# A small two-block image kernel: own shift products for two of four images, shared ones for the other two, fillers, halved last products and new engine orders

## The reference

```python
x = x + attention(_gn(x))   # qkv (1x1), 8 heads of 12 channels, l2-normalized q and k,
                            # 12x12 channel attention with temperature, softmax, projection + bias
x = x + ffn(_gn(x))         # 1x1 in, 8x8-patch real FFT times a filter, inverse FFT,
                            # 3x3 depthwise convolution, gelu(x1) * x2, 1x1 out
```

## Time and profile before

| | us |
|---|---|
| median of 3 runs | 68.55 (68.52 to 69.21) |
| profiled execution, its own time | 68.19 |
| span of its trace (first to last instruction) | 66.4 |
| TensorE busy | 59.0 |
| VectorE busy | 40.9 |
| ScalarE busy | 34.5 |
| GpSimd busy | 22.2 |

### The profile page before, as it was taken

The page is one execution under the profiler, slowest core; times in us unless marked ns, Lnnn a source line. Parts: engine busy times, 40 slices in busy tenths (PEclk is TensorE's granted clock), DMA queues, the critical chain, the costliest instruction groups (busy, mean ns, idle before and its releaser), DMA issues.

```text
span 66.4 us, 1346 instructions
## 1 busy us (share of the span) xinstructions
PE 59.0 (89%) x428; PEld 48.4 (73%) x428; DVE 40.9 (62%) x158; ACT 34.5 (52%) x88; POOL 22.2 (33%) x39
## 2 busy tenths in 40 slices
PE   3939999999999999999999999999999999979200
PEld 3929999979796989989899999889759651403000
DVE  0000035696416979699999859899998698870000
ACT  0710300037089466953519998968598614442920
POOL 3031003915160314330301599829397540000000
PEclk9999999999999999999999999999999999999999
DMA  0899999996000000000000000000000701520392
GB/s 0 239 340 268 368 239 260 247 262 197 25 0 0 5 0 0 0 0 10 0 0 5 0 0 0 10 0 0 15 5 20 236 11 35 149 93 0 83 307 84
DMA packets 3427, 5.83 MB, mean 88 GB/s; under 512 B 642, under 2 KB 1820, under 8 KB 3420
## 3 DMA queue, kind: packets, MB, share of 16 engines
q1 hardware_dynamic: 3004, 5.45, 28.8%
q10 hardware_dynamic: 416, 0.29, 1.9%
HBM read 4.04 MB, written 1.57 MB: 85 GB/s over the span
## 4 chain that ended last, share of the span: by engine, by line
PE 69%; DVE 7%; DMA 5%; ACT 4%; issue 3%; ACTq 1%; DVEq 1%; POOLq 1%; POOL 1%; SPq 1%
PE CH L735 26%; PE CV L735 18%; PE AB L735 15%; PE VB L735 10%; DMA XT<-in_xT 5%; DVE AB L723 3%; ACT X L538 2%; DVE AB L704 2%; DVE GT L729 2%; ACTq L272 1%; POOL CD L493 1%; POOLq L272 1%; DVEq L272 1%; ACT GE L578 1%; SPq L414 1%
## 5 line engine op out<-in xcount | busy, mean ns | idle before, releaser
L735 PE MATMUL AB<-CST,XT 128*97 128x128 f32 x64 | 9.4, 294 | 1.0 <-DMA XT<-in_xT 1.0
L486 POOL TENSOR_TENSOR ZP<-ZP,TURNED 128x512 f32<-128x512 f32 x6 | 7.6, 1271 | 5.9 <-ACT TURNED L533 5.8
L735 PEld LDWEIGHTS AB<-CST,XT 128*97 128x97 f32 x64 | 8.1, 178 | 1.3 <-DMA XT<-in_xT 1.3
L514 ACT ACTIVATE XF<-AB 97x512 f32<-97x512 f32 x8 | 4.7, 587 | 3.9 <-PE AB L735 3.9
L735 PEld LDWEIGHTS CH<-CST,ZA 128*128 128x128 f32 x48 | 5.8, 192 | 0.9 <-issue 0.8
L735 PE MATMUL CH<-CST,ZA 128*128 128x80 f32 x48 | 6.3, 275 | 0.0
L538 ACT ACTIVATE X<-CV,ST 96x512 f32<-96x512 f32 x6 | 3.8, 678 | 4.7 <-PE CV L735 4.7
L735 PE MATMUL CV<-X,AT 96*96 96x512 f32 x12 | 6.0, 597 | 0.0
L597 DVE COPY GI<-CH 97x97 f32<-97x97 f32 x2 | 0.5, 252 | 8.1 <-PE CH L735 8.1
L532 ACT ACTIVATE TURNED<-ZQ 64x512 f32<-64x512 f32 x6 | 3.8, 628 | 2.0 <-DVE ZQ L688 1.9
L475 POOL TENSOR_TENSOR RN<-NRM,POWER 96x2 f32<-96x2 f32 x4 | 2.8, 690 | 5.9 <-DVE NRM L639 5.9
(11 more groups left out here) (154 smaller groups left out, 130.2 us busy)
## 6 DMA issues: line engine op xcount, KB each, us to landing
X<-in_x SPq DMA_DIRECT2D x4, 384.0 KB, 8.3
out<-X SPq DMA_DIRECT2D x8, 192.0 KB, 2.2
XT<-in_xT SPq DMA_DIRECT2D x3, 388.0 KB, 6.3
XT<-in_xT SPq DMA_DIRECT2D x2, 194.0 KB, 3.2
WTS<-in_weights SPq DMA_DIRECT2D x1, 168.0 KB, 7.4
X<-GT SPq DMA_DIRECT2D x4, 32.0 KB, 1.9
WTS<-in_weights ACTq DMA_DIRECT2D x1, 126.9 KB, 5.4
LATE<-in_late SPq DMA_DIRECT2D x1, 109.5 KB, 6.8
```

The costliest lines, as they stand in the source:

```text
L486: ins = nc.gpsimd.tensor_tensor(ZP[:, b - 1, of], ZP[:, b - 1, of], TURNED[:, b - 1, of], ALU.add)
L514: nc.scalar.activation(XF[:, b, HALF * h:HALF * (h + 1)], bank[0:C1, :], ACT.Copy).then_inc(a_free, 1)
L735: return nc.tensor.matmul(o, lhsT, rhs, start=start, stop=stop)
```

## The change

Images 0 and 1 each get a shift product of their own (one SHIFT column each), so `shift.0` no longer waits for image 1's statistics. Images 2 and 3 share not only the shift but also the statistics product, the variance operations and the power. Two fillers (each one product of ones, two passes) stand before gram.1 and two more before attend.1. The final products of images 3 and 0 are issued half by half, each behind its own gate. All four orders are new: gram.0 comes ahead of spec.0.1, gram.2 and gram.3 behind shift.0.

```diff
 PE_ORDER = steps("""
-    spec.0.1 gram.0 gram.1 stats.0 gram.2 stats.1 gram.3 stats.2 shift.0 stats.3 spec.2.1 project.0
-    project.1 spec.1.0 logits.0 shift.2 logits.1 spec.3.1 softmax.0 project.2 setup.0 softmax.1 project.3
-    logits.2 spec.1.1 attend.0 logits.3 mix.0 attend.1 softmax.2 second.0 mix.1 spec.3.0 group.0 second.1
-    attend.2 spec.0.0 mix.2 group.1 softmax.3 fold.0 second.2 filter.0.0 group.2 spec.2.0 fold.1
-    filter.0.1 attend.3 filter.1.0 mix.3 fold.2 filter.1.1 edge.1.0 second.3 filter.2.0 edge.1.1 group.3
-    back.1.0 filter.2.1 back.1.1 edge.2.0 fold.3 edge.2.1 base.1.0 filter.3.0 filter.3.1 back.2.0
-    base.1.1 back.2.1 edge.3.0 final.1 edge.3.1 back.3.0 base.2.0 back.3.1 base.2.1 final.2 base.0.0
-    base.3.0 base.3.1 base.0.1 final.3 final.0
+    gram.0 spec.0.1 stats.0 fill.0 fill.0 gram.1 shift.0 gram.2 project.0 stats.1 gram.3 spec.0.0 stats.2
+    setup.0 logits.0 shift.1 spec.2.1 project.1 shift.2 softmax.0 logits.1 project.2 project.3 spec.2.0
+    attend.0 softmax.1 logits.2 mix.0 logits.3 second.0 fill.0 fill.0 attend.1 softmax.2 group.0 mix.1
+    spec.3.0 second.1 spec.1.0 softmax.3 attend.2 fold.0 group.1 mix.2 filter.0.0 second.2 filter.0.1
+    fold.1 spec.1.1 group.2 attend.3 filter.1.0 spec.3.1 filter.1.1 mix.3 fold.2 edge.1.0 second.3
+    filter.2.0 edge.1.1 group.3 back.1.0 filter.2.1 back.1.1 edge.2.0 fold.3 edge.2.1 filter.3.0 back.2.0
+    filter.3.1 base.1.0 back.2.1 edge.3.0 base.1.1 edge.3.1 final.1 back.3.0 base.2.0 back.3.1 base.2.1
+    final.2 base.0.0 base.3.0 base.0.1 base.3.1 final.3.0 final.3.1 final.0.0 final.0.1
 """)
 ACT_ORDER = steps("""
-    spec.0.1 shift.0 spec.2.1 tk.0 tk.1 shift.2 kl.0 spec.1.0 kl.1 tk.2 softmax.0 spec.3.1 tk.3 softmax.1
...
-    edge.3.0 final.1.0 final.1.1 edge.3.1 gelu.2.0 gelu.2.1 final.2.0 final.2.1 gelu.3.0 gelu.3.1
+    shift.0 tk.0 spec.0.1 spec.0.0 shift.1 tk.1 kl.0 shift.2 spec.2.1 softmax.0 tk.2 tk.3 kl.1 q1.0
...
+    swap.3.1 edge.3.0 edge.3.1 final.1.0 final.1.1 gelu.2.0 gelu.2.1 final.2.0 final.2.1 gelu.3.0
...
 DVE_ORDER = steps("""
-    gram.0 var.0 gram.1 var.1 gram.2 norm.0 norm.1 gram.3 var.2 var.3 norm.2 norm.3 project.0 project.1
...
-    gate.2.0 gate.2.1 rows.3 cols.3 gate.3.0 gate.3.1
+    gram.0 var.0 norm.0 gram.1 var.1 gram.2 gram.3 project.0 norm.1 var.2 logits.0 norm.2 rq.0 norm.3
...
+    gate.2.1 cols.3 rows.3 gate.3.0 gate.3.1
...
 POOL_ORDER = steps("""
-    var.0 var.1 var.2 var.3 logits.0 logits.1 logits.2 spread.0 logits.3 group.0 group.1 group.2 zsum.1.0
-    zsum.1.1 group.3 cdiff.1 rdiff.1 zsum.2.0 cdiff.2 zsum.2.1 zsum.3.0 rdiff.2 zsum.3.1 cdiff.3 rdiff.3
+    var.0 var.1 var.2 logits.0 logits.1 logits.2 logits.3 group.0 group.1 group.2 zsum.1.0 zsum.1.1
+    cdiff.1 group.3 rdiff.1 zsum.2.0 zsum.2.1 rdiff.2 zsum.3.0 cdiff.2 zsum.3.1 spread.0 cdiff.3 rdiff.3
...
-            nc.gpsimd.memset(SHIFT[:], 0.0).then_inc(zero_set, 1)
+            nc.gpsimd.memset(SHIFT[:, PAIRED, :], 0.0).then_inc(zero_set, 1)
...
+                    if b == PAIRED:
+                        ins = nc.gpsimd.tensor_tensor(pair(RSTD), pair(VAR), POWER[:], ALU.pow)
...
+                        mean, square = ps[0:C, P_GROUP:P_GROUP + 4:2], ps[0:C, P_GROUP + 1:P_GROUP + 4:2]
+                        v.tensor_scalar(pair(NEGMEAN), mean, -1.0, None, ALU.mult).then_inc(negmean_set, 1)
+                        dve.wait_ge(negmean_set, b + 1)
+                        then(v.tensor_tensor(pair(NEGVAR), pair(NEGMEAN), mean, ALU.mult))
+                        v.scalar_tensor_tensor(pair(VAR), pair(NEGVAR), EPS, square, ALU.add, ALU.add).then_inc(var_set, 1)
...
+                        nc.scalar.activation(WA[C:C1, b, :], ps[C:C1, 2 * C:4 * C], ACT.Copy).then_inc(wa_set, 1)
+                        nc.scalar.activation(WVU[:, b, C:C1], ps[0:C, P_U:P_U + 1], ACT.Copy).then_inc(u_set, 1)
...
-                    dve.wait_ge(wa_set, 2 * (b // 2 + 1))
+                    dve.wait_ge(wa_set, b + 1 if b < PAIRED else B)
...
-                    pe.wait_ge(gate_set, max(through(GATE_STEPS, ("gate", of, 0)), through(GATE_STEPS, ("gate", of, 1))))
+                    pe.wait_ge(gate_set, max(through(GATE_STEPS, ("gate", of, h)) for h in halves))
...
-                    for h in range(2):
+                    for h in halves:
...
-                    pe.wait_ge(shift_set, b + 2)
-                    pe.wait_ge(negmean_set, b + 2)
+                    pe.wait_ge(shift_set, b + 1)
...
+                        mm(ps[C:C1, 2 * C:4 * C], SHIFT[:, b, 0:1], WTS[0:C, W_QK:W_QK + 2 * C])
+                        mm(ps[0:C, P_U:P_U + 1], WTS[0:C, W_VT:W_VT + C], SHIFT[:, b, 0:1]).then_inc(shift_sum, 1)
```

More of the change, by code:

```diff
@@ L219 @@
-    final.3.0 final.3.1 final.0.0 final.0.1
+    shift.0 tk.0 spec.0.1 spec.0.0 shift.1 tk.1 kl.0 shift.2 spec.2.1 softmax.0 tk.2 tk.3 kl.1 q1.0
+    spec.2.0 softmax.1 aas.0 kl.2 q1.1 softmax.2 kl.3 spec.3.0 aas.1 weigh.0 q1.2 fold.0 softmax.3
+    weigh.1 aas.2 spec.1.0 fold.1 spec.1.1 q1.3 weigh.2 spec.3.1 fold.2 swap.1.0 aas.3 edge.1.0 swap.1.1
+    edge.1.1 swap.2.0 weigh.3 edge.2.0 fold.3 swap.2.1 edge.2.1 table.0 gelu.1.0 swap.3.0 gelu.1.1
+    swap.3.1 edge.3.0 edge.3.1 final.1.0 final.1.1 gelu.2.0 gelu.2.1 final.2.0 final.2.1 gelu.3.0
@@ L220 @@
+    gelu.3.1 final.3.0 final.3.1 final.0.0 final.0.1
 """)
 DVE_ORDER = steps("""
-    gram.0 var.0 gram.1 var.1 gram.2 norm.0 norm.1 gram.3 var.2 var.3 norm.2 norm.3 project.0 project.1
[L223 to L226, removed]
@@ L227 @@
-    gate.2.0 gate.2.1 rows.3 cols.3 gate.3.0 gate.3.1
+    gram.0 var.0 norm.0 gram.1 var.1 gram.2 gram.3 project.0 norm.1 var.2 logits.0 norm.2 rq.0 norm.3
+    project.1 softmax.0 logits.1 setup.0 attend.0 rq.1 project.2 project.3 softmax.1 logits.2 mix.0
+    logits.3 attend.1 second.0 rq.2 rq.3 softmax.2 mix.1 group.0 attend.2 second.1 softmax.3 group.1
+    mix.2 attend.3 filter.0.0 second.2 filter.0.1 group.2 filter.1.0 mix.3 filter.1.1 second.3 filter.2.0
+    group.3 filter.2.1 cols.1 rows.1 filter.3.0 filter.3.1 gate.1.0 gate.1.1 rows.2 cols.2 gate.2.0
@@ L248 @@
 FINAL_STEPS = [s for s in ACT_ORDER if s[0] == "final"]
-PROJECTED = [s for s in PE_ORDER if s[0] == "final"]
+PAIRED = 2
+PROJECTED = [("final", s[1], h) for s in PE_ORDER if s[0] == "final" for h in s[2:] or range(2)]
 SP_ORDER = [s for b in range(1, B) for s in [("move", b, 0), ("move", b, 1)] * (b < GROUPS) + [f for f in FINAL_STEPS if f[1] == b]] + [
@@ L329, in col, with pair @@
             return ST[0:C, b, which:which + 1]
+        def pair(which):
+            return ST[0:C, PAIRED:PAIRED + 2, which]
         CH = [ctx.enter_context(nc.psum_tensor(f"CH{i}", [128, 512], F32)) for i in range(2)]
@@ L471, in _ @@
                     pool.wait_ge(var_set, b + 1)
[L472 removed]
+                    if b == PAIRED:
+                        ins = nc.gpsimd.tensor_tensor(pair(RSTD), pair(VAR), POWER[:], ALU.pow)
+                    else:
+                        ins = nc.gpsimd.tensor_tensor(col(b, RSTD), col(b, VAR), POWER[:, 0:1], ALU.pow)
                 elif step[0] == "logits":
@@ L535, in _ @@
                     h = step[2]
-                    act.wait_ge(f_full, 2 * PROJECTED.index(("final", b)) + h + 1)
+                    act.wait_ge(f_full, through(PROJECTED, step))
                     act.wait_ge(bias_set, b + 1)
@@ L540, in _ @@
                 elif step[0] == "shift":
[L541 to L545, removed]
+                    act.wait_ge(shift_sum, b + 1)
+                    if b == PAIRED:
+                        for n in range(2):
+                            at = GELU_AT + 32 * n
+                            nc.scalar.activation(WA[C:C1, b + n, :], ps[at:at + 1, 2 * C:4 * C], ACT.Copy).then_inc(wa_set, 1)
+                        nc.scalar.activation(WVU[:, b:b + 2, C:C1], ps[0:C, P_U:P_U + 2].unsqueeze(2), ACT.Copy).then_inc(u_set, 1)
+                    else:
+                        nc.scalar.activation(WA[C:C1, b, :], ps[C:C1, 2 * C:4 * C], ACT.Copy).then_inc(wa_set, 1)
+                        nc.scalar.activation(WVU[:, b, C:C1], ps[0:C, P_U:P_U + 1], ACT.Copy).then_inc(u_set, 1)
                 elif step[0] == "q1":
@@ L613, in _ @@
                 elif name == "norm":
-                    dve.wait_ge(negmean_set, b + 1)
-                    dve.wait_ge(pool_done, through(POOL_ORDER, ("var", b)))
-                    if b == 0:
+                    n = min(b, PAIRED)
+                    dve.wait_ge(negmean_set, n + 1)
+                    dve.wait_ge(pool_done, through(POOL_ORDER, ("var", n)))
+                    if b < PAIRED:
+                        v.tensor_tensor(SHIFT[:, b, 0:1], col(b, NEGMEAN), col(b, RSTD), ALU.mult).then_inc(shift_set, 1)
+                    elif b == PAIRED:
                         dve.wait_ge(zero_set, 1)
-                    at = 32 * (b % 2)
-                    v.tensor_tensor(SHIFT[:, b // 2, at:at + 1], col(b, NEGMEAN), col(b, RSTD), ALU.mult).then_inc(shift_set, 1)
```

(5 more changed lines are left out.)

27 lines of the change are left out of this document (17 added, 10 removed).

## The result

The changed kernel takes 74.13 us (median of 6 runs, 73.05 to 74.84); the kernel before, on the same chips, 69.16 (68.52 to 69.74). The ratio is 1.074 (95% interval 1.067 to 1.080), and by the medians it is 5.0 us slower. All ratios here are of the undisturbed, quicker runs of each kernel, while medians are of all its runs. The direction was as forecast, the size twice the forecast's 2.4 us and outside its range. The profiled execution took 73.94 us, its span is 72.1 us against 66.4, 5.7 more.

What follows compares the result with a forecast made beforehand. TensorE was taken as near full, VectorE nearly so from 28.61 us on. Added work less the earlier shift.0 (+3.3), halves (-0.6) and regained waits (-0.3) gave +2.4 us: forecast 71.0 us, range 69.0 to 72.8.

Steps and rivals of the forecast that it cites:

- The chain: Start: GpSimd's wait for the WTS transfer, landing at 11.0, holds var.0 and SHIFT, so shift.0 starts at 12.9 us.
- The ledger: TensorE behind shift.0: 4.0 us of added work, less 0.7 for the earlier shift.0, so final.3 starts 3.3 us later.
- what the orders regain: Middle of TensorE's work: new orders trim between 0 and 2.4 us of waits, taken as 0.3.
- The halves: End of the kernel: final products split by halves let the last copies come earlier, 0.6 us gained.
- the term of the clock: Loss from TensorE's clock falling in the gap before shift.0: not in the sum, priced only in the third rival.
- the third rival: TensorE's clock falls to half pace in the gap before shift.0, costing 1.2 to 2.1 us: 72.6 us, chance 0.18.
- the length of the hole: TensorE between gram.1 and shift.0: idle from 10.4 to 12.9 us, 2.5 us.
- The rival on the faster side: Start: if the WTS transfer landed before 8.6 us, shift.0 is ready as gram.1 ends: about 67.3 us, chance 0.08.

Runs made afterwards that it cites:

- e1_early_pow: The changed kernel with GpSimd's wait for mix_in and its copy to WVU moved behind var.1: 67.58 us, ratio to the kernel before 0.986.
- e2_keep_busy: The changed kernel with 18 more fillers between gram.1 and shift.0 on TensorE: 73.03 us, ratio to the kernel before 1.065.
- b2_gram_first: The kernel before with only gram.0 put ahead of spec.0.1 on TensorE: median 70.77 us, ratio 0.980 from its quick runs alone.
- e3_grams_first: The changed kernel with gram.2 and gram.3 put back ahead of shift.0 on TensorE alone: 73.78 us, ratio to the kernel before 1.061.
- e4_early_transfer: The changed kernel with the transfer that mix_in counts issued right behind XT of image 1: 68.09 us, ratio to the kernel before 0.990.
- e1_whole_final: e1_early_pow with final.3 and final.0 whole again, each behind both gates: 68.14 us, ratio to the kernel before 0.997.

## Why the prediction was wrong in size and right in kind

**The chain was right.** Transfer, copy, warming pow, var.0, SHIFT, shift.0, with gram.2 and gram.3 behind it, stands in the trace link by link. shift.0 came at 13.36 instead of the 12.9 of the working, as the transfer landed at 11.43 and not at 11.0.

**The ledger was nearly right.** To filter.0.0 it expected 15.0 + 2.8 = 17.8 us at full pace; e1_early_pow, where the clock doesn't fall, took 18.21; where those 0.4 us come from wasn't followed up. By its own prices three shift steps against two are 0.5 us and not 0.6, which makes the gap 0.1 wider. From filter.0.0 to final.3 it expected 32.5 less what the orders regain (0.3); to final.3.1 it was 32.04 (34.13 to 66.17). The halves were put at 0.6 and brought 0.56. Without the clock the change measures -0.2 for shift.0 (13.59 to 13.36), +3.2 to filter.0.0 and +0.2 from there to final.3.0, so 3.2 us; the forecast had 2.4, and 0.46 for the later landing and 0.4 to filter.0.0 make up the difference.

**The step that failed is the term of the clock, which the sum put at nothing.** It stood only in the third rival, with a chance of 0.18 and a price of 1.2 to 2.1 us. It cost 2.56 us in the profiled execution. The mean granted clock over the span was 0.938 to 0.976 in the six runs, of which some lies behind the last matmul; in the two runs at 0.976 half pace can't have cost more than 72 x 0.024 = 1.7 us, and their spans (71.9 and 72.5 us) are no shorter, so 2.56 is the price in one execution, and in those two more of the loss lay elsewhere. Two mistakes stand behind the low chance. First, the length of the hole: I had gram.1 end at 10.4 and TensorE idle for 2.5 us. It ended at 9.2 and was idle for 4.15. The working let gram.0 run at half pace to its end and spec.0.1 and the fillers at half pace too; with gram.0 started at 3.46, spec.0.1 already took 1.04 us, not 1.7. Part of this is the scatter of the start, as in e1_early_pow spec.0.1 took 1.60 us and gram.1 ended at 10.16. I counted an earlier end of gram.1 as harmless, since shift.0 waits anyway. It was harmless for shift.0 and decisive for the clock. Second, I took the absence of a hole in the trace of before as no evidence either way, where the trace had a hint, which the rival names: the first work of the program ran at half pace. By the rule of the Trainium skill ("TensorE: Matmul & The Clock Gate", "Part 1: The HAM clock gate") an idle TensorE goes back to 1.2 GHz; the trace agrees, 0.50 granted from 12.0 us on. A hole of several microseconds should have been forecast with that fall, not beside it. The measured price gives 71.0 + 2.56 = 73.6.

**The price was also too low,** as I took one Gram product, or a slow stretch as long as the 4.2 us at the start. At half pace went everything from 13.36 to between 18.5 and 19: shift.0 (1.01 instead of 0.58), gram.2, project.0, stats.1 and about half of gram.3.

**The rival on the faster side named the right point.** It had the landing of the transfer as what decides, at 8.6 us. With the landing at 8.75 the kernel took 68.09 us, 1.0% less than before; the 67.3 was a little low, with a hole of 1.08 us left.

**What the change did bring.** Without the wait, and without its fillers, it is 2.8% faster than the kernel before (2.1% by the medians). But the old orders with gram.0 first and the copy behind var.1 reach 2.7% (1.8% by the medians), with neither own shift products, nor pairing, nor halves. What own shift products, pairing and the new orders add could not be told from nothing here; they weren't tried one by one.

## What to carry to other kernels

A wait that costs nothing today can stand one step from the path: before an engine's steps are drawn forward, walk every queue that they pass through from its first line, set-up code included, and write down what lands when. A hole in TensorE's work is to be priced with the work behind it at half pace, and an estimate of when the work ahead of it ends matters as much as when the hole closes. When the orders are changed, a single misplaced wait or transfer can decide more than the orders do: here moving one copy or one transfer was worth 6 us of 74.

## What the runs showed of the hardware that was not expected

The same transfer, issued at the same time by the same queue, lands up to 3.2 us apart from one execution to the next: GpSimd's copy of WVU started at 11.01 (before), 11.43 (after), 11.10, 11.96, 13.16 and 9.92 us in the profiled executions of kernels that issue it alike. gram.1's XT was there by 6.41 in one and only at 8.78 in another (e2_keep_busy). An order that rests on a landing inherits this scatter. b2_gram_first ran from 67 to 80 us as one kernel, with granted clocks from 0.997 to 0.836; that late landings brought its clock down is likely, but no trace shows it. The kernel before isn't free of it: one of its runs took 71.55 us at 0.959.

The granted clock fell after holes far shorter than the 4.15 us one: in e3_grams_first after a hole of 1.35 us in a thin stretch, and it stayed down for 13 us (15 to between 28 and 29), although TensorE was reported busy all the while. Yet it stayed at 1.00 after the 1.08 us of e4_early_transfer, and in e2_keep_busy after 1.54 us in which no weights were loaded ahead of gram.1. The length of the hole alone doesn't tell, and from these runs alone one can't say what does. Nor does the mean granted clock alone give the time: a run of e1_whole_final at 0.953 took 67.65 us, the fastest of its twelve. And the half pace of the first matmuls doesn't show in the granted clock: gram.0's sixteen weight loads took 2.25 us in the changed kernel under a granted 1.00.
